# A masked one-hot with one transpose, a weight split moved within each head, and norm sums in strips

## The reference

```python
h = einsum('bct,bcd->bdt', x, weights[condition])          # 32x32 per sequence
q = rms_norm(h @ Wq + bq, gq); k = rms_norm(h @ Wk + bk, gk); v = h @ Wv + bv   # 512 -> 4096
attn = softmax(einsum('bhqd,bhkd->bhqk', q, k) / sqrt(128))
x = x + einsum('bhqk,bhkd->bhqd', attn, v).reshape(B, S, 4096) @ Wo + bo
```

## Time and profile before

| | us |
|---|---|
| three runs, median | 857.16 (854.96, 857.16, 857.17) |
| the profiled execution | 855.03 |
| its span, first to last instruction | 853.2 |
| mean granted clock of the matrix engine | 0.996 |
| busy: matrix engine, weight loads | 827.1, 670.3 |
| busy: VectorE, GpSimd, ScalarE | 589.7, 448.4, 347.1 |

### The profile page before, as it was taken

The page is one execution under the profiler, slowest core; times in us unless marked ns, Lnnn a source line. Parts: engine busy times, 40 slices in busy tenths (PEclk is TensorE's granted clock), DMA queues, the critical chain, the costliest instruction groups (busy, mean ns, idle before and its releaser), DMA issues.

```text
span 853.2 us, 15304 instructions
## 1 busy us (share of the span) xinstructions
PE 827.1 (97%) x6105; PEld 670.3 (79%) x6105; DVE 589.7 (69%) x636; ACT 347.1 (41%) x404; POOL 448.4 (53%) x433
## 2 busy tenths in 40 slices
PE   5799999999999999999999999999999999999998
PEld 4578877777777777777888888888888888888466
DVE  3888888888888888888556456466584767553441
ACT  2465555445555555554413323442421414222420
POOL 4989874432222222110069994569999999000330
PEclk9899999999999999999999999999999999999999
DMA  6016111111111111220011110141511011346501
GB/s 179 26 51 177 54 43 49 50 49 49 49 49 49 49 49 49 74 99 1 1 50 50 49 50 0 50 98 49 99 28 41 32 49 52 124 172 222 137 25 75
DMA packets 77529, 56.54 MB, mean 66 GB/s; under 512 B 25548, under 2 KB 60716, under 8 KB 77372
## 3 DMA queue, kind: packets, MB, share of 16 engines
q1 hardware_dynamic: 76528, 55.67, 21.9%
q10 hardware_dynamic: 972, 0.48, 0.3%
HBM read 52.32 MB, written 3.82 MB: 66 GB/s over the span
## 4 chain that ended last, share of the span: by engine, by line
PE 86%; DVE 8%; issue 3%; ACT 2%; DMA 1%; DVEq 0%; ACTq 0%
PE psum L650 14%; PE psum L652 14%; PE psum L651 14%; PE psum L696 11%; PE psum L698 10%; PE psum L697 10%; PE psum L792 7%; DVE w_lo L1238 3%; PE psum L731 2%; DVE sumsq L1326 1%; PE psum L897 1%; DVE qk_sb L1307 1%; PE psum L672 1%; DVE t_lo L1284 1%; DMA cond_nat<-in_cond_w 1%
## 5 line engine op out<-in xcount | busy, mean ns | idle before, releaser
L1457 DVE TENSOR_TENSOR acc<-psum,acc 128x512 f32<-128x512 f32 x64 | 44.2, 691 | 98.4 <-PE psum L652 98.4
L404 POOL TENSOR_TENSOR w_raw<-w_raw 128x256 f32<-128x256 f32 x32 | 23.6, 738 | 159.7 <-DMA w_raw<-in_wk 159.2
L696 PE MATMUL psum<-t_hi,w_hi 128*128 128x512 f32 x256 | 103.6, 405 | 1.4 <-DVE qk_sb L1299 0.9
L650 PE MATMUL psum<-wv_hi,mix_hi 128*128 128x512 f32 x256 | 100.4, 392 | 0.2 <-DVE wv_lo L1332 0.2
L652 PE MATMUL psum<-wv_hi,mix_lo 128*128 128x512 f32 x256 | 99.6, 389 | 0.0
L697 PE MATMUL psum<-t_lo,w_hi 128*128 128x512 f32 x256 | 99.6, 389 | 0.0
L651 PE MATMUL psum<-wv_lo,mix_hi 128*128 128x512 f32 x256 | 99.6, 389 | 0.0
L698 PE MATMUL psum<-t_hi,w_lo 128*128 128x512 f32 x256 | 99.6, 389 | 0.0
L650 PE MATMUL psum<-wo_hi,attn_hi 128*128 128x512 f32 x224 | 87.1, 389 | 0.0
L651 PE MATMUL psum<-wo_lo,attn_hi 128*128 128x512 f32 x224 | 87.1, 389 | 0.0
L652 PE MATMUL psum<-wo_hi,attn_lo 128*128 128x512 f32 x224 | 87.1, 389 | 0.0
(11 more groups left out here) (247 smaller groups left out, 1815.8 us busy)
## 6 DMA issues: line engine op xcount, KB each, us to landing
w_raw<-in_wq SPq DMA_DIRECT2D x32, 256.0 KB, 2.9
w_raw<-in_wk SPq DMA_DIRECT2D x32, 256.0 KB, 3.2
wv_raw<-in_wv SPq DMA_DIRECT2D x8, 1024.0 KB, 5.4
toep<-kpad_dram SPq DMA_DIRECT2D x2, 4096.0 KB, 15.1
wo_raw<-in_wo SPq DMA_DIRECT2D x7, 1024.0 KB, 5.4
x_nat<-in_x SPq DMA_DIRECT2D x4, 512.0 KB, 6.5
acc<-in_x SPq DMA_DIRECT2D x1, 2048.0 KB, 10.9
out_dram<-o_stage SPq DMA_DIRECT2D x8, 256.0 KB, 2.0
```

The source lines that it names most:

```text
L650: mm(out, lh, rh, start=(n == 0), stop=False)
L696: mm(bank(n), wh, hi[:, c, tok], start=(i == 0), stop=False)
L1457: v.tensor_tensor(acc[:, g, :], bank(6 + g % 2), acc[:, g, :], ALU.add).then_inc(acc_ok, 1)
```

## The change

- One-hot: `cond_f` is filled with -1 and only sequence g*4+q is written in row q, so that each copy of the one-hot picks a quarter of the sequences and the others become zero. The two products then give the block-diagonal layout, and one transpose writes `mix_w` whole. `cond_nat` is now SP's first transfer, no longer the second of ScalarE's queue.
- Head 0's weight split is cut in two: three blocks before the first mix group is evicted, four at the place where all seven were.
- GpSimd does all four groups of token sums, and `combine(1, ...)` comes after them. VectorE's fourth group is gone.
- In each head `split_lo(h + 1)` stands behind u4, ahead of the square add and c12. It waits for the same semaphores.
- Norm sums: only the diagonal 32x32 blocks are computed, each strip of 32 weight columns at its own tile position; one instruction reads the k sums.

```diff
@@ sync @@
+            sp.dma_start(cond_nat[:], cond_w.rearrange("n c d -> n (c d)")).then_inc(cond_in, 16)
             load_x(0)
@@ gpsimd @@
+            for n in range(4):
+                token_sums(n)
             combine(1, 1, 32, early=True)
-            for n in range(3):
-                token_sums(n)
@@ tensor @@
-            for n in range(2):
-                last = mm(bank(2 + n), ones[:, :], sumsq[:, 1, HALF * n:HALF * n + HALF], start=True, stop=True)
+            for b in range(BPG):
+                last = mm(bank(2, G * SEQ)[quadrant(b), :], ones[:, quadrant(b)],
+                          sumsq[:, 1, :].rearrange("p (g b k) -> p b g k", g=G, b=BPG)[:, b], start=True, stop=True,
+                          tile_position=(0, 32 * b))
...
             for g in range(G):
-                last = mm(bank(5)[:, g:g + 1], sumsq[:, 0, P * g:P * g + P], ones[:, 0:1], start=True, stop=True)
+                for b in range(BPG):
+                    last = mm(bank(5)[quadrant(b), g:g + 1], sumsq[:, 0, P * g + SEQ * b:P * g + SEQ * b + SEQ],
+                              ones[:, 0:1], start=True, stop=True, tile_position=(0, 32 * b))
@@ scalar @@
+            act.wait_ge(w_in[0], 32)
+            split_hi(0, 0, 3).then_inc(whi0_ok, 1)
             for n in range(4):
                 mix_out(n)
             act.wait_ge(ws_start, 4)
-            split_hi(0, 0, 7).then_inc(whi_ok, 1)
+            split_hi(0, 3, 7).then_inc(whi0_ok, 1)
@@ vector @@
+            v.memset(cond_f[:], -1.0).then_inc(zero_ok, 1)
...
-            v.tensor_copy(cond_f[:], cond_i[:]).then_inc(condf_ok, 1)
+            own = cond_f[:].rearrange("n q b -> n (q b)")
+            own = bass.AP(own.tensor, own.offset, [list(own.ap[0]), [BATCH + 1, BPG], [BPG, G]])
+            v.tensor_copy(own, cond_i[:].rearrange("n (g q) -> n q g", q=BPG)).then_inc(condf_ok, 1)
...
-            v.transpose(mix_t[:], bank(0, 1024).rearrange("p (c d) -> p d c", d=32)).then_inc(mixt_ok, 1)
...
-            for b in range(BPG):
-                last = v.tensor_copy(mix_w[quadrant(b), :, quadrant(b)],
-                                     mix_t[quadrant(b)].rearrange("p d (g b) -> p g d b", b=BPG)[:, :, :, b])
+            v.transpose(mix_w[:].rearrange("p g (b d) -> p d (g b)", d=32),
+                        bank(0, 1024).rearrange("p (c d) -> p d c", d=32)).then_inc(mixw_ok, 1)
...
+            dve.wait_ge(whi0_ok, 1)
+            first_lo(0, 3)
...
-            split_lo(0, 0)
+            dve.wait_ge(whi0_ok, 2)
+            first_lo(3, 7).then_inc(wlo_ok, 1)
...
                 post("u4", h, slot)
+                if not last_head:
+                    dve.wait_ge(p4_mm, h)
+                    split_lo(h + 1, 1 - slot)
                 if not (isinstance(h, int) and h == 1):
                     add_squares(1, h - 1, k_sq, k_sum)
                 post("c12", h, slot)
                 if last_head:
                     split_v(0)
-                else:
-                    dve.wait_ge(p4_mm, h)
-                    split_lo(h + 1, 1 - slot)
```

More of the change, by code:

```diff
@@ L121, in build_program @@
             [("mix_hi", [P, KC, TOK], F32R), ("mix_lo", [P, KC, TOK], F32R)])
-        ((mix_w, mix_t, cond_nat, cond_i, cond_f, cond_no, onehot, prm_nat), (a_sum, b_sum, gated, k_sb),
+        ((mix_w, cond_nat, cond_i, cond_f, cond_no, onehot, prm_nat), (a_sum, b_sum, gated, k_sb),
          (toep0,), (ax_hi, ax_lo), (scores,)) = overlay(
-            [("mix_w", [P, G, P], F32), ("mix_t", [P, 32, BATCH], F32), ("cond_nat", [NCOND, 32 * 32], F32),
-             ("cond_i", [NCOND, BATCH], I32), ("cond_f", [NCOND, BATCH], F32), ("cond_no", [NCOND, 1], F32),
+            [("mix_w", [P, G, P], F32), ("cond_nat", [NCOND, 32 * 32], F32),
+             ("cond_i", [NCOND, BATCH], I32), ("cond_f", [NCOND, BPG, BATCH], F32), ("cond_no", [NCOND, 1], F32),
              ("onehot", [NCOND, BPG, BATCH], F32),
@@ L196, in build_program @@
         const_ok, sel_const = sem("const_ok"), sem("sel_const")
-        condf_ok, hot_ok, mixt_ok = sem("condf_ok"), sem("hot_ok"), sem("mixt_ok")
+        condf_ok, hot_ok, whi0_ok = sem("condf_ok"), sem("hot_ok"), sem("whi0_ok")
         zero_ok = sem("zero_ok")
@@ L201, in build_program @@
         mix_mm, mixhi_ok, mixlo_ok, mixf_ok = (sem(n) for n in ("mix_mm", "mixhi_ok", "mixlo_ok", "mixf_ok"))
-        t_ok, t3_ok, thi_ok, tlo_ok = sem("t_ok"), sem("t3_ok"), sem("thi_ok"), sem("tlo_ok")
+        t_ok, thi_ok, tlo_ok = sem("t_ok"), sem("thi_ok"), sem("tlo_ok")
         gqk_ok = sem("gqk_ok")
@@ L674, in _ @@
                 last.then_inc(mix_mm, 1)
-            pe.wait_ge(mixt_ok, 1)
             pe.wait_ge(const_ok, 2)
@@ L828, in _ @@
                 value_group(0, g)
-            pe.wait_ge(var_ok, 5)
+            pe.wait_ge(var_ok, 2)
             attend(0, first=True)
@@ L965, in _ @@
             act.dma_start(cond_i[:], every_partition(cond_idx, BATCH, NCOND)).then_inc(cond_in, 16)
-            act.dma_start(cond_nat[:], cond_w.rearrange("n c d -> n (c d)")).then_inc(cond_in, 16)
             act.dma_start(prm_nat[:, 9, :], ssm_c.rearrange("h n two -> h (n two)")).then_inc(c_in, 16)
@@ L1015, in t_hi_out @@
                 chunks, tok = ((slice(0, 2), 0), (slice(0, 2), 1), (slice(2, 4), 1), (slice(2, 4), 0))[n]
-                act.wait_ge(t_ok, 9 + n)
-                act.wait_ge(t3_ok, n + 1)
+                act.wait_ge(t_ok, 13 + n)
                 sc.activation(t_hi[:, chunks, halves(tok)], mix_f[:, chunks, halves(tok)], ACT.Copy).then_inc(thi_ok, 1)
@@ L1243, in _, with first_lo @@
             dve.wait_ge(mixw_mm, 1)
-            v.transpose(mix_t[:], bank(0, 1024).rearrange("p (c d) -> p d c", d=32)).then_inc(mixt_ok, 1)
-            dve.wait_ge(mixt_ok, 1)
-            dve.wait_ge(zero_ok, 1)
-            for b in range(BPG):
-                last = v.tensor_copy(mix_w[quadrant(b), :, quadrant(b)],
-                                     mix_t[quadrant(b)].rearrange("p d (g b) -> p g d b", b=BPG)[:, :, :, b])
-            last.then_inc(mixw_ok, 1)
+            v.transpose(mix_w[:].rearrange("p g (b d) -> p d (g b)", d=32),
+                        bank(0, 1024).rearrange("p (c d) -> p d c", d=32)).then_inc(mixw_ok, 1)
+            def first_lo(a, b):
+                return v.tensor_tensor(w_lo[0][:, a:b, :].rearrange("p b n -> p (b n)"),
+                                       w_raw[0][:, a + 1:b + 1, :].rearrange("p b n -> p (b n)"),
+                                       w_hi[0][:, a:b, :].rearrange("p b n -> p (b n)").bitcast(F32), ALU.subtract)
+            dve.wait_ge(whi0_ok, 1)
+            first_lo(0, 3)
             def mix_out(n):
@@ L1269, in _ @@
             CH1, CH2 = slice(0, 2), slice(2, 4)
-            b11, b12, b21, b22 = (mix_f[:, chunks, HALF * n + 3 * P:HALF * n + HALF] for chunks in (CH1, CH2) for n in range(2))
-            dve.wait_ge(mixf_ok, 4)
-            dve.wait_ge(mixhi_ok, G)
-            v.tensor_tensor(b11, b12, b11, ALU.subtract).then_inc(t3_ok, 1)
-            dve.wait_ge(t3_ok, 1)
-            v.tensor_tensor(b12, b22, b12, ALU.subtract).then_inc(t3_ok, 1)
-            v.tensor_tensor(b22, b22, b11, ALU.subtract).then_inc(t3_ok, 1)
-            dve.wait_ge(t3_ok, 3)
-            v.tensor_tensor(b21, b21, b22, ALU.subtract).then_inc(t3_ok, 1)
             def t_low(n):
@@ L1379, in _ @@
             dve.wait_ge(vk_mm, 1)
-            for b in range(BPG):
-                src = bank(2, 1024)[quadrant(b), :].rearrange("p (g k) -> p g k", g=G)[:, :, quadrant(b)]
-                v.tensor_scalar(var_k[quadrant(b)], src, 1.0 / INNER, RMS_EPS, ALU.mult, ALU.add).then_inc(var_ok, 1)
+            v.tensor_scalar(var_k[:].rearrange("p g k -> p (g k)"), bank(2, G * SEQ), 1.0 / INNER, RMS_EPS,
+                            ALU.mult, ALU.add).then_inc(var_ok, 1)
             dve.wait_ge(vq_mm, 1)
             v.tensor_scalar(var_q[:], bank(5, G), 1.0 / INNER, RMS_EPS, ALU.mult, ALU.add).then_inc(var_ok, 1)
-            dve.wait_ge(var_ok, 5)
+            dve.wait_ge(var_ok, 2)
             v.scalar_tensor_tensor(inv_norm[:], var_k[:], float(HD), repeat(var_q[:], 2, 32),
```

5 lines of the change are left out of this document (3 added, 2 removed).

## The result

The changed kernel takes 847.75 us (median of six runs, 846.92 to 848.66); the kernel before, run beside it, 857.16 (six runs, 854.96 to 857.69). The ratio is 0.990, with a 95% interval of 0.989 to 0.992: faster, by more than the 851.0 of the forecast and inside its range. The profiled execution took 848.52 us, its span is 846.7.

A forecast was written before the change was run, and what follows sets the result against it. The matrix engine, busy 97%, was taken as the bound. Head 4 +4.8, loop -7.8 and norm sums -2.1 make -5.1 us: 849.9 from the profiled execution, 852.1 from the median, middle 851.0; range 845 to 858.

The forecast's parts named there:

- the loop's gain: Head loop: w_lo made two microseconds earlier, behind u4, gains 7.8 us (from 3 to 9.8).
- GpSimd's longer chain: GpSimd's queue up to head 4: eight more operations make head 4's sums of weights end at 72.3 us.
- the clock at head 4: Behind the wait before head 4: clock falls, 11 products at 0.43 us instead of 0.23, +2.2 us.
- the base: Starting time for the terms: the profiled execution's 855.03 us or the median 857.16; the forecast took the middle.
- The opening: Up to head 1: cond_nat's landing -2.4 us, four copies removed -1.55; mixing near 9.4, p1 about 21.5.
- 8 x 0.8 = +6.4: GpSimd before head 4: four token-sum operations and four of head 1's sums join its chain, +6.4 us.
- Head 4: Head 4's first product at 76.1 us, its third +4.8 us later than before (from +1 to +7).
- the 0.8 of slack: Head loop: c21 ends at 313.0 us, the product waiting for it is due at 313.8.
- Rival B: Head loop: w_lo ahead of the square add makes c21 late, the loop gives nothing, 858.8 us; chance 0.14.
- The norm sums: Norm sums near 379.73 us: strips side by side take 0.7 and 0.8 us, -2.1 (from 0 to -2.4).
- The sum: Whole kernel: +4.8 -7.8 -2.1 = -5.1 us, giving 849.9 from the profiled execution, 852.1 from the median.
- the opening's gain at head 1: At head 1: 2.2 us kept of the gain at p1, less 0.8 for the clock, leaving -1.4.

The follow-up runs named there:

- the experiment with the fourth group: The changed kernel with the fourth group of token sums (four operations) given back from GpSimd to VectorE: 844.74 us.
- head 1's sums came first: The changed kernel with head 1's sums of weights on GpSimd ahead of the token sums again, as before the change: 847.60 us.
- The norm edit's kernel: The kernel before with one edit, the norm sums in strips: 856.05 us, ratio 0.9986.
- the split place alone: The kernel before with one edit, split_lo behind u4 in each head: 847.38 us, ratio 0.989.
- the small work: GpSimd's exponentials and reciprocal for the convolution's parameters; put behind later heads' sums, against the changed kernel: 843.45 us.
- the line for cond_nat: cond_nat's load moved to the head of SP's queue: 855.10 us in the kernel before, 841.31 with old opening and small work later.

## Why the prediction was right

The mechanism held: the loop's gain is the change, GpSimd's longer chain is its price, and it falls due at head 4. Three sizes were off, the rest of GpSimd's chain, the clock at head 4 and the base; the forecast of 851.0 came out 3.3 us too high. Point by point:

- **The opening.** Mixing starts at 9.47 (9.4 predicted), but two terms were off against each other: cond_nat landed at 0.74+2.1 = 2.8 (3.6 taken), so that the products now wait for cond_i (in at 3.0) and their chain starts 3.0 us earlier instead of 2.4, and the transpose takes 1.90 instead of 1.25. The 4.8 us that cond_nat took in the trace of before was itself an unlucky one: four other traces with that opening have 3.9 to 4.1. The rows of L1427 were no measure for it: they write with a stride too, from and into another layout. Token sums start at 14.53 (14.65), p1 at 21.99 (21.5), `dqk` at 33.69 (34.2).
- **GpSimd's chain.** Without idle from 14.53 on, as predicted. The term that was mis-sized is "8 x 0.8 = +6.4", with 0.3 more for blocked operations: from the first token sum to the end of head 4's sums it took 50.9 us before and 56.0 after, +5.1. The eight operations themselves were not cheaper. They stand from 24.72 to 33.69, 9.0 us, since three of them were blocked and took 1.6 to 1.7 instead of 0.73, two of them these:

```profile
28.71 1.72 POOL L405 TENSOR_TENSOR w_raw<-w_raw 128x256 f32<-128x256 f32 x1
30.39 1.72 POOL L406 TENSOR_TENSOR w_raw<-w_raw 128x256 f32<-128x256 f32 x1
```

  What the prediction took as unchanged, the rest of the chain, became 3.9 us shorter, because fewer of its operations were blocked: the other twelve token sums took 10.2 instead of 11.1, the steps from `dqk` to head 2's sums 1.2 instead of 1.7, and all from there to the end of head 4's sums 35.6 instead of 38.1, with seven operations that took a microsecond or so too long instead of ten. The 0.69 per operation of the experiment with the fourth group is such a net figure too. So head 4's sums ended at 70.5 instead of 72.3.
- **Head 4.** The first product comes at 74.41 (76.1) and the third, for p6, at 78.79 (81.2): +2.4 on before instead of +4.8. 1.7 of the difference is the chain. Most of the other 0.7 is the fall of the clock, priced at 2.2 on top of the wait. It is not on top: from the start of w_lo to p6 it takes 6.46 us with the clock fallen (72.33 to 78.79), and 6.46 us as well where head 1's sums came first and the clock stayed at 1.00 (71.32 to 77.78). There c21, queued behind the late w_lo, is waited for 1.37. The prediction named c21 as running beside the fall; it covers all of the fall, not half.
- **The loop.** 7.3 us over the same 25 rounds in the traces (7.8 predicted); by medians the edit is worth 9.3 to 10.1. The weight loads wait for c21 eight times, 4.0 us in all, so the 0.8 of slack was about right. Rival B fell.
- **The norm sums.** -2.46 on the chain (-2.1 predicted, with 1.5 us for what took 1.20). The bound of -2.4 was just missed; from the last scores to the end it is -2.1. The Trainium skill, "TensorE: Matmul & The Clock Gate", section "Wait — 56ns, not 53.3ns?", would have started the 64 records of the q part no closer than about 25 ns. They took 0.74 us, under 12 ns apart, in four strips:

```profile
375.70 0.74 PE L827 MATMUL psum<-ones,sumsq 128*32 128x1 f32 x64
```

- **The sum.** Between the profiled executions it is -6.5 where -5.1 was predicted. That the medians differ by 9.4 comes from the base: the profiled execution of before lay 2.1 under its median and that of after 0.8 over its own. I had taken the middle of two bases. For before, the median was the right one and 852.1 the number that the working gave; the trace's 849.9 was nearer to the result by chance.
- **A step argued wrongly, without harm.** I took the opening's gain at head 1 from one execution of before. The norm edit's kernel has the old opening and head 1 at 47.38, 0.17 ahead of the changed kernel's 47.55. So the 3.1 us at head 1 that two traces show can all be the luck of one of them, in cond_nat's landing and in the clock. That the opening edit as a whole gives nothing is what the experiments with and without it say: +2.7, +1.0 and 0.0 us. With the fourth group back on VectorE it gives 2.0 and 3.9.

Still open is what makes the runs of one kernel differ: those with the split at its old place vary by 2.9 to 5.5 us (12 runs each) and the split place alone by 1.1 (6 runs), but others with the new place by up to 4.2 (5 runs). It also leaves open the size of the split place's effect, 9.3 to 10.1 us by medians but 7.1 to 8.6 between heads 4 and 31 of single traces; in two of the three pairs the profiled executions themselves differ by only 8.3 and 6.9. And behind the rounds with GpSimd's bias additions a round takes 10.46 us in the changed kernel and 10.42 in five others, such as the one with the fourth sums back, about 1 us over the loop; why was not looked for.

## What to carry to other kernels

Moving a step off an engine that looks idle on the average (GpSimd, 53% busy) is only free where its own queue has slack before its next deadline; follow that queue to the first result that somebody waits for, and count operations there. While such a deadline binds, a gain made ahead of it can only lengthen the wait in front of it, so clear the deadline first. The new opening with the fourth group on VectorE fits this (worth 2.0 us with the small work in place, 3.9 without); the line for cond_nat, 2.0 and 2.1 by medians, neither shows it nor speaks against it. And do not take the start of one stage from one trace: the same opening code put head 1 anywhere between 47.38 and 50.66. And in a loop whose rounds all wait a little for one value, ask which of the instructions ahead of its producer nobody is waiting for: putting the square addition behind w_lo was worth more than everything else in this change.

## What the runs showed of the hardware

- A transpose of 128x1024 on VectorE from PSUM takes 1.25 us into a contiguous tile and 1.90 us straight into the block-diagonal one. It replaced both the transpose and four copies (1.53), so it still pays; the freed time was 0.9 us, not 1.55. Where the four copies fell beside GpSimd's sums of weights they took 3.12 and 2.83, so with early weights the one transpose saves more (mixing at 9.47 against 11.92 and 11.74).
- The same kind of stop does not always bring the clock down. Ahead of p1 the matrix engine was idle for 3.06 us in one kernel and 3.10 in another, and the granted clock stayed at 1.00 in the first and fell to 0.50 in the second; in the changed kernel 2.06 us before p1 were followed by 0.50, and 3.28 us before 36.60 by 1.00; with head 1's sums first, 2.06 us before p1 were followed by 1.00. What the fall costs: from p1 to head 1's scores it takes 21.4 us in two kernels with the old transpose and copies whose clock stayed at 1.00, and 22.1 to 23.3 in the five of them whose clock fell; near 810 us it was 2.1. So an idle stretch is a risk of 1 to 2 us here, not a price, and one profiled execution shows one throw.
- Products in four strips of the array run side by side: on the chain the k sums went from 1.98 to 0.62 us for the same result, though their records doubled (x4 to x8). Those of one column follow each other at under 12 ns: the q sums went from 1.68 to 0.58, though their records quadrupled (x16 to x64).
- VectorE and GpSimd slow each other far from the opening too, and it varies which of them pays. b_lo falls beside GpSimd's eight bias additions near 800 us. In the changed kernel it takes 2.56 and the additions 12.00; with head 1's sums first, where it starts beside the last of them, it takes 3.47 and they take 9.95:

```profile
798.32 12.00 POOL L634 TENSOR_TENSOR acc<-acc,fb_rows 128x512 f32<-128x512 f32 x8 [11.31 <-DMA fb_rows<-in_ffn_b]
...
806.62 2.56 DVE L1511 TENSOR_TENSOR b_lo<-b_all,b_hi 128x2048 fp32r<-128x2048 f32 x1
```

```profile
795.51 9.95 POOL L634 TENSOR_TENSOR acc<-acc,fb_rows 128x512 f32<-128x512 f32 x8 [10.98 <-DMA fb_rows<-in_ffn_b]
```
